# Two expert products and the bias product move from the first stage of a batch into the steps of its second

## The reference, cut to what matters

```python
xn = _layernorm(x, axis=-1)
s = _L0_attn_ref(xn, wq, w_down, wk_up, wv_up, wo)      # 16 heads, rope, page mask
# inside _L0_ffn_ref, t = xn as (tokens, d):
w = jax.nn.softmax(masked, axis=1)                      # 2 of the 8 weights are not zero
eh = jax.nn.silu(jnp.einsum('td,edh->teh', t, ew1) + eb1[None])
eo = jnp.einsum('teh,ehd->ted', eh, ew2) + eb2[None]
y = t + jnp.einsum('te,ted->td', w, eo)
...
x = x + s * _silu(y)
```

## Time and profile before

| what | value |
|---|---|
| median of 3 runs | 665.55 us (663.73 to 666.62) |
| profiled execution, first to last instruction | 663.7 us |
| PE busy | 607.3 us (92%) |
| DVE busy | 467.0 us (70%) |
| ACT busy | 354.4 us (53%) |
| chain that ended last | PE 70%, DVE 13%, issue 12%, ACT 2% |
| mean granted TensorE clock | 0.971 of full speed |

### The profile page before, as it was taken

How to read it: one execution, slowest core, us unless ns; L and a number is a source line. 1 busy time by engine, 2 the same in 40 slices (tenths; PEclk the granted TensorE clock), 3 DMA queues, 4 the chain that set the end, 5 groups by cost and what they waited for, 6 DMA issues and landing times.

```text
span 663.7 us, 12438 instructions
## 1 busy us (share of the span) xinstructions
PE 607.3 (92%) x4116; PEld 448.6 (68%) x4116; DVE 467.0 (70%) x1199; ACT 354.4 (53%) x507; POOL 18.6 (3%) x20
## 2 busy tenths in 40 slices
PE   2569999999999999999999999999999999999895
PEld 1448855787567865678557875788656885578643
DVE  6677866787568866798667865698757875687502
ACT  2123456643766347754576438653576445763573
POOL 0000000000000100001000000001000000000000
PEclk9758999999999989999999999999999998999999
DMA  5810002100120002200021001200021001200000
GB/s 170 210 43 2 3 13 61 27 1 19 38 60 1 18 1 49 46 1 18 21 51 25 1 18 45 50 1 18 1 67 28 2 17 25 51 22 2 19 1 16
DMA packets 21798, 20.93 MB, mean 32 GB/s; under 512 B 4545, under 2 KB 14450, under 8 KB 21778
## 3 DMA queue, kind: packets, MB, share of 16 engines
q1 hardware_dynamic: 21778, 20.67, 12.9%
HBM read 5.45 MB, written 2.10 MB: 11 GB/s over the span
## 4 chain that ended last, share of the span: by engine, by line
PE 70%; DVE 13%; issue 12%; ACT 2%; SPq 1%; DMA 1%; DVEq 0%; POOLq 0%; POOL 0%; ACTq 0%
PE bank L500 15%; PE bank L580 10%; PE ring L517 7%; PE ring L562 7%; PE bank L446 5%; PE bank L447 5%; PE bank L448 5%; PE bank L517 5%; DVE row_max L861 5%; PE ring L565 2%; DVE acc L908 2%; PE ring L566 2%; PE bank L462 1%; ACT probs L683 1%; PE bank L478 1%
## 5 line engine op out<-in xcount | busy, mean ns | idle before, releaser
L683 ACT ACTIVATE probs<-ring 128x768 f32<-128x768 f32 (+1 forms) x192 | 158.9, 880 | 79.7 <-PE ring L562 48.8
L861 DVE TENSOR_REDUCE row_max<-ring 128x2 f32<-128x256 f32 (+1 forms) x192 | 152.3, 819 | 13.1 <-PE ring L517 13.0
L643 ACT ACTIVATE eh<-bank,bias_cols 128x512 f32<-128x512 f32 x128 | 87.8, 686 | 136.9 <-PE bank L448 134.9
L500 PE MATMUL bank<-ew_sb,eh 128*128 128x128 f32 x1024 | 125.8, 276 | 2.4 <-DVE x_lo L786 2.4
L500 PEld LDWEIGHTS bank<-ew_sb,eh 128*128 128x128 f32 x1024 | 120.1, 192 | 5.6 <-issue 3.8
L517 PE MATMUL ring<-k_head,q_stack 108*128 108x256 f32 (+2 forms) x384 | 93.4, 344 | 12.3 <-DVE row_max L861 11.2
L517 PEld LDWEIGHTS ring<-k_head,q_stack 108*128 108x128 f32 x384 | 66.7, 194 | 37.0 <-DVE row_max L861 24.8
L580 PE MATMUL bank<-probs,v_cols 128*32 128x512 f32 (+3 forms) x1024 | 88.0, 442 | 0.4 <-ACT probs L683 0.4
L908 DVE SCALAR_TENSOR_TENSOR acc<-bank,gate_w,acc 128x128 f32<-128x128 f32 x224 | 63.1, 345 | 32.3 <-PE bank L500 32.1
L856 DVE TENSOR_REDUCE row_max<-bank 128x1 f32<-128x128 f32 (+3 forms) x128 | 58.9, 487 | 32.6 <-PE bank L517 31.7
L562 PE MATMUL ring<-q_stack,k_head 128*128 128x512 f32 (+1 forms) x256 | 71.8, 395 | 3.5 <-ACT probs L683 3.5
(11 more groups left out here) (115 smaller groups left out, 659.4 us busy)
## 6 DMA issues: line engine op xcount, KB each, us to landing
k_stack<-roped_hi SPq DMA_DIRECT2D x64, 64.0 KB, 2.0
q_stack<-roped_hi SPq DMA_DIRECT2D x64, 64.0 KB, 2.0
k_stack<-roped_lo SPq DMA_DIRECT2D x32, 64.0 KB, 2.0
q_stack<-roped_lo SPq DMA_DIRECT2D x32, 64.0 KB, 2.0
out<-out_sb SPq DMA_DIRECT2D x8, 256.0 KB, 2.3
x_all<-in_L_attn_x SPq DMA_DIRECT2D x4, 448.0 KB, 6.9
probs<-in_L_ffn_ew SPq DMA_DIRECT2D x1, 1024.0 KB, 5.8
q_stack<-neg_rows SPq DMA_DIRECT2D x32, 16.0 KB
```

The lines of the kernel that those rows point to most:

```text
L500: last = mm(ps[:, t * E:(t + 1) * E], eh[:, s % EH_RING, t * P:(t + 1) * P], ew2_sb[:, e, f, :], start=(f == 0), stop=(f == HALVES - 1))
L643: nc.scalar.activation(eh[:, s % EH_RING, :], wide[s % 2][:], ACT.Silu, bias=bias_cols[:, s:s + 1]).then_inc(hidden_done, 1)
L683: nc.scalar.activation(probs[:, n % 2, r:r + 2, lo:T], ring[:, r:r + 2, lo:T], ACT.Exp, scale=SCALE).then_inc(exp_done, 1)
L861: V.tensor_reduce(row_max[:, g, i, 2 * pair:2 * pair + 2], ring[:, 2 * (m % 2):2 * (m % 2) + 2, 0:(i + 1) * P], AX, ALU.max).then_inc(max_ ...
```

## The change

Three entries of the tables move, no instruction is added or removed. `layer2` 6 and `layer2` 7 leave the end of stage B and stand before `pv` 0 and before `pv` 1; `expert_bias` leaves its place between `proj` 0 and `proj` 1 and stands after `pv` 2.

```diff
-    layer2_at = {4: 0, 6: 1, 7: 2, 9: 3, 11: 4, 13: 5, 15: 6}
+    layer2_at = {4: 0, 6: 1, 7: 2, 9: 3, 11: 4, 13: 5}
...
-    return seq + [("layer2", NE - 1), ("neg_max", 3), ("proj", 0), ("expert_bias", 0), ("proj", 1)]
+    return seq + [("neg_max", 3), ("proj", 0), ("proj", 1)]
...
-    before_pv = {5: [("heads", 0)], 8: [("heads", 1)]}
-    after_pv = {0: [("proj", 2), ("split", 0), ("proj", 3)], 1: [("split", 1), ("stack", 0)], 4: [("stack", 1)],
-                7: [("stack", 2)], 10: [("stack", 3)], NSTEP: [("values", 0), ("negate", 0)]}
+    before_pv = {1: [("layer2", 6)], 2: [("layer2", 7)], 5: [("heads", 0)], 8: [("heads", 1)]}
+    after_pv = {0: [("proj", 2), ("split", 0), ("proj", 3)], 1: [("split", 1), ("stack", 0)],
+                3: [("expert_bias", 0)], 4: [("stack", 1)], 7: [("stack", 2)], 10: [("stack", 3)], NSTEP: [("values", 0), ("negate", 0)]}
```

## The result

The changed kernel takes 671.34 us (median of 4 runs, 671.19 to 671.42) against 666.09 for the kernel before on the same chip; ratio 1.0081, 95% interval 1.0062 to 1.0100. It is slower by 5.3 us. The profiled execution spans 669.3 us, 5.6 more than before, and was timed at 671.19: 1.9 us of a time lie outside the span.

A forecast was written before the change was run, and what follows sets the result against it. PE, busy 92% of the span, was taken to set the pace at both places. From the profiled 663.7 us, +3.1 for exchanged idle time and +5.8 for clock falls gave 672.6, stated as 672.5, own range 669 to 675.5.

The forecast's parts named there:

- The gap: End of stage B: PE idles 2.57 us before neg_max 3, waiting for DVE's negation; scores 0 starts 3.69 us earlier.
- What comes back: First steps of stage C: two layer2 products and half of expert_bias put pv 3 4.13 us later relative to scores 0.
- the guessed 0.05: Stage C: 0.05 us added to the 3.56 us of two layer2 insertions for a changed hand-over to pv.
- Net of the order: Each batch with a next one: 4.13 later less 3.69 earlier, +0.44 us per batch, +3.1 over seven.
- The last batch: Without x_cols or proj; pv 3 was to come within 0.1 us of before, counted as 0.
- DVE and the queues: Stage C: acc of layer2 6 delays split 1 and k_head, but k_head is done before its first use at 335.3.
- The room: k_head on DVE: done before 332.5, first use moving to 335.3; before the change it was 0.98 us ahead.
- The clock: Batch boundaries: six falls to 1.2 GHz instead of two, 1.45 us each, +5.8 us; bounds -2.9 and +8.7.
- The sixth fall: Last batch: one clock fall expected there, because two idle pieces lie close together; 1.45 us per fall.
- rival 1: Batch boundaries: clock as before, only idle time exchanged; 666.8 us, or 668.7 from the median; chance 0.27.
- The sum: Whole kernel: 663.7 of the profiled execution + 3.1 + 5.8 = 672.6 us, stated as 672.5.
- two terms that were too large: Whole kernel: the new order's exchange of idle time, +3.1 us, and the further clock falls, +5.8 us.

The follow-up runs named there:

- e5: The changed kernel with expert_bias one step earlier, behind pv 1 instead of pv 2; 677.54 us, ratio 1.0174 to the kernel before.
- e4: The kernel before with four matmuls of unused result in PE's 0.96 us wait ahead of proj 0; 663.04 us, ratio 0.9959 to the kernel before.
- e10: The changed kernel with four matmuls of unused result in front of PE's wait for negate 3; 664.86 us, ratio 0.9989 to the kernel before.
- e3: The changed kernel with ten matmuls of unused result in front of PE's wait for negate 3; 665.40 us, ratio 0.9998 to the kernel before.
- e2: The kernel before with expert_bias alone moved behind pv 2; 657.03 us, ratio 0.9869 to the kernel before.
- e8: e2 plus a product 32 rows deep, result overwritten, between proj 0 and proj 1; 672.02 us, ratio 1.0087 to the kernel before.
- e9: e2 plus a product 128 rows deep, result overwritten, between proj 0 and proj 1; 662.41 us, ratio 0.9945 to the kernel before.
- e1: The changed kernel with layer2 6 put back between x_cols and neg_max 3; 655.14 us, ratio 0.9844 to the kernel before.
- e6: e1 with negate 3 placed ahead of x_cols; 652.29 us, ratio 0.9790 to the kernel before.

## Why the prediction was right

- **The gap.** Predicted 2.57 us behind x_cols, released by DVE's negation; it is 2.48, since PE starts 0.06 us after the release and not 0.15. The same shorter release holds at proj 1. Scores 0 starts 3.88 us earlier, not 3.69.
- **What comes back.** Pv 3 was to stand 4.13 us later relative to scores 0; in batch 4 it is 13.55 against 9.42 in the same batch before, 4.13. Each layer2 adds 1.77 to 1.78 us between scores and pv without a wait, so the guessed 0.05 was not needed, and half of expert_bias lies under the wait on exp, as forecast (0.56 us of it come back, not 0.5); e5 took that cover away and lost 0.5 us per batch.
- **Net of the order.** +0.22 to +0.28 per batch, not +0.44; 1.3 us in all by the spans, about 1.5 by e4 and e10, not 3.1. The two release times, 0.09 and 0.10 us too long, are nearly the whole error.
- **The last batch.** Counted as nothing; from the last matmul of layer1 to the end it is 44.0 us for 44.1.
- **DVE and the queues.** k_head never releases PE in the loop; its wait for the DMA shrank from 1.87 us to 0.77 and cost nothing. The room was overrated: k_head is done 1.51 us ahead of its first use, where I had 2.8 and before it was 0.98.
- **The clock.** Five of seven boundaries were forecast and five fell. The sixth fall, in the last batch, did not come. A fall costs 1.3 to 1.45, and the clock's share is 4.1 us, not 5.8. That it is the clock is shown by e3 and e10: filling the gap takes all of it away. The reasoning behind the five, a chance in proportion to the idle piece, was too simple, and that exactly five came is partly luck: e5 has the same gap and fell at six. The falls of the kernel before hung on the thin product as well: e2 keeps the gap, drops the product and has none, and of e8 and e9 only the thin one falls. In the changed kernel no such product stands near the gap; with 2.48 us of idle time it fell five times, with 1.38 left (e10) not once in the profile. Whether the transposes behind the gap have a part in it is not tested.
- **The case for rival 1.** That PE was busy for only 1.81 us of 656 to 660 at clock 1.00 was weak evidence: between 662 and 664 the clock fell. The window showed only that the fall had not come yet.
- **The advice of the Trainium skill** ("TensorE: Matmul & The Clock Gate", "Why this matters for your kernels") to keep gaps below its limit did not protect this kernel: 2.48 us of idle time, below the limit, went with a fall at five of seven boundaries.
- **The sum.** 672.6 was a span, as it was built on one; I took the 1.9 us between span and median for further falls, when every run shows such a difference between its own time and its span (1.8 to 3.3 us). The execution profiled before, of 663.7 us span, was thus not the shortest run of 663.73 us but one nearer to the median. The forecast of 672.5 is near the measured 671.34 partly because this omission made up for two terms that were too large: by spans I forecast +8.9 and 5.6 came.

## What to carry to other kernels

Moving work off a wait moves the wait: before taking a product from behind a short step, replay what the engine then waits for, and leave one product there if a chain through other engines is that long (here e1 and e6, 1.6% and 2.1% faster than before, with the same instructions). Ask of each moved step by itself what it leaves behind; here the bias alone was worth 1.3%, a third of it by the clock, layer2 7 added about 0.3 us per batch to that, and layer2 6 turned the sum negative. Try to fill or split an idle piece of PE when the granted clock drops behind it; four matmuls with no use were worth 0.9% here (e10).

## What the runs showed of the hardware

A product 32 rows deep behind a gap of 0.96 us went with falls of the granted clock to 1.2 GHz (e8), one 128 rows deep of equal columns did not (e9; 9.6 us between the two kernels, 7 of them put down to the clock). In this kernel PE's idle time alone thus did not decide. The thin product also took longer: 0.37 us more per batch at full clock. And matmuls whose results are thrown away were better than free here: e4 adds four of them at each boundary and is 0.4% faster.
